# Block 0's weighted sums over channels: from VectorE to TensorE, with diagonal matrices from ScalarE

## The chip, the cores and the metric

The kernel runs on one core of one Trainium2 chip. The metric is the time of one execution on the device, in microseconds (us). The engines are called by their names: TensorE (PE in the rows; PEld is its weight load), VectorE (DVE), ScalarE (ACT), GpSimd (POOL) and SyncE (SP). Each runs its own list of instructions in order, and they wait for each other at semaphores.

## What is computed

A transformer layer with a residual of four channels: attention, then an MLP, then a layer with a matrix of signs. What matters here is the MLP's read. Ahead of it the residual is updated channel by channel with the attention's output (`rat_write`), and the read makes two outputs, each a weighted sum over the four channels with its own weight for each feature, normalized over the features:

```python
def rat_read(res, W, gamma, beta, num_outputs):
    b, l, _ = res.shape
    x = res.reshape(b, l, H, C)                # H = 512 features, C = 4 channels
    y = jnp.einsum('blhc,hoc->bloh', x, W)     # num_outputs = 2 in the MLP
    mu = y.mean(-1, keepdims=True)
    var = y.var(-1, keepdims=True)
    yn = (y - mu) * jax.lax.rsqrt(var + EPS)
    yn = yn * gamma.reshape(num_outputs, H) + beta.reshape(num_outputs, H)
    return yn.reshape(b, l, num_outputs * H)
```

There are 2 x 1024 tokens. Everything is f32; the large products are made from a high and a low part in a rounded f32 format.

## The kernel before

Features lie on the 128 partitions, tokens along the free axis. The tokens are worked in `NB` = 4 blocks of `T` = 512. The program has four phases: setup, read, attention, and `block_phase`, to which the change belongs. In `block_phase` each block `v` has a **first write** (update of the residual with the attention's output, then the read), an **inner product** (`inner`: gate and up projections, product, down projection, 16 steps), a **second write** (update with the MLP's output) and the product with the signs (`signs`). For blocks 1 to 3 the first write is laid between the steps of another block's products by the class `Between`. For block 0 there is no other work: its first write stands alone, after the attention and ahead of `inner(0)`.

The order in each engine is the order in which the Python generators issue. Block 0's first write goes like this:

- TensorE: `expansions` (factors for the update, banks `X0` and `X1`), then `walls(1)` (60 matmuls that belong to block 1 and fill banks 0 to 4 of the eight PSUM banks), then `read(0)`: for each of the two outputs `o` the mean over features (matmuls of `ones_h` with `Y`, line 1657), then the same with the squares for the variance (line 1666).
- VectorE: `factors`, then for each channel `c` the update in `channel` (lines 2052 to 2060, for the last channel 2067 to 2072) on a piece `hidden` of 128 x 2048, and behind it the sums: eight instructions of 128 x 512, one for each of two outputs and four groups `hc` of 128 features, which multiply the piece by the weight `RW[:, hc, o, c]` and add it to `Y` (lines 2109 and 2111). Behind channel 2 stands `small_lows` (line 2080), which frees the bank `SMALL` (4). At the end `Y - mean` (2122), times the reciprocal deviation (2127), gamma and beta (2130), and the low part `ZL` (2136).
- ScalarE: the exponentials of the update (1870), `take_walls(1)`, which copies banks 0 to 3 to `out_1` (1890), four weight DMAs for `inner(0)` (1903 to 1908), of which the first waits for the last update (`wr` 4), and the third for the store of channel 2's piece and the sums of channel 2 (`y` 3); then squares (1911), reciprocal deviation (1918, 1920), the high part `ZH` (1926).
- GpSimd: loads and stores of the pieces. Block 0 has three buffers for four channels, so channel 3's load (line 1430) waits for the store of channel 0's piece and for channel 0's sums (`y` 1). The stores of channels 1 to 3 (line 1436) stand behind it in the queue.

Semaphores: `wr` counts updated pieces, `y` the sums (channels 0 to 2, then output 0 and output 1 of the last), `ym` means, `yc` subtractions, `sq` squares, `yv` variances, `rs` reciprocal deviations.

## Time and profile before

| | us |
|---|---|
| median of 3 runs | 2212.17 |
| lowest and highest of them | 2210.51, 2214.36 |
| the profiled execution's own time | 2214.25 |
| its span (first to last instruction) | 2212.4 |
| mean granted TensorE clock | 0.959 of full speed |

The profile is of one execution. All starts and durations are read from it, in us from the start of its span. What lies around the span (2214.25 against 2212.4) is not seen in it. The chain of waits is the path that ended last, followed back from the last instruction; a wait that is not on it costs nothing. The granted clock is TensorE's: 1.00 is 2.4 GHz, 0.50 is 1.2 GHz, and a value between them is a slice in which it changed.

### The profile page before, as it was taken

The page shows a single profiled execution, that of the slowest core. Times are in us where ns is not written, and L with a number is a line of the kernel's source. Part 1 is how long each engine was busy: PE and PEld are TensorE (multiplying, and loading weights), DVE is VectorE, ACT ScalarE, POOL GpSimd, SP SyncE. Part 2 cuts the span into 40 slices and gives each one's busy share as a digit, 9 for nine tenths or more (in the row PEclk, how much of TensorE's full clock was granted, in tenths as well). Part 3 has the DMA queues.
Part 4 walks back from the last instruction along what each step waited for, and adds up shares of the span by engine and source line. Part 5 has one row for each costly group of instructions (what it writes and reads, how often), then busy time and mean ns, then how long its engine had stood idle before and what let it go on. Part 6 is the DMA issues. An engine that isn't in the chain of part 4 may idle for free.

```text
span 2212.4 us, 25095 instructions
## 1 busy us (share of the span) xinstructions
PE 1981.1 (90%) x9562; PEld 1378.9 (62%) x9562; DVE 1415.1 (64%) x1563; ACT 978.9 (44%) x1376; POOL 423.3 (19%) x325
## 2 busy tenths in 40 slices
PE   2789897999999996289989999999999999989997
PEld 0344456666566553157767777777777677766786
DVE  3677767677777755958657638758639658468100
ACT  3656652787788875044145233143341162431100
POOL 1000004676555550000000001110001000011111
PEclk9899997999999997699999999999999999999999
DMA  8848346686666743246666657777658677559675
GB/s 198 186 110 187 91 102 207 238 289 235 239 239 223 265 171 128 100 165 235 230 238 225 248 186 218 233 243 261 227 191 234 207 263 277 224 162 258 156 183 136
DMA packets 180924, 453.87 MB, mean 205 GB/s; under 512 B 64320, under 2 KB 64576, under 8 KB 165440
## 3 DMA queue, kind: packets, MB, share of 16 engines
q1 hardware_dynamic: 146160, 313.31, 42.3%
q0 software_dynamic: 32480, 128.46, 20.9%
q10 hardware_dynamic: 2160, 10.43, 1.3%
q8 instruction: 79, 1.29, 0.2%
q14 instruction: 45, 0.37, 0.1%
HBM read 304.80 MB, written 147.32 MB: 204 GB/s over the span
## 4 chain that ended last, share of the span: by engine, by line
PE 44%; DVE 7%; DMA 5%; ACT 4%; issue 2%; SPq 0%; POOL 0%; DVEq 0%; POOLq 0%; ACTq 0%
PE ps L1788 16%; PE ps L1598 8%; PE ps L1600 7%; PE ps L1599 7%; DMA sign_h<-sign_h_scratch 2%; DMA up<-up_s_scratch 2%; PE ps L1657 1%; PE ps L1666 1%; PE ps L1695 1%; ACT L1817 1%; PE ps L1618 1%; DVE Y L2111 1%; PE ps L1707 1%; DVE DL_attn L2018 0%; DVE E_attn L2023 0%
## 5 line engine op out<-in xcount | busy, mean ns | idle before, releaser
L1788 PE MATMUL ps<-XH,sign_h 128*128 128x512 f32 x768 | 308.9, 402 | 13.5 <-DMA sign_h<-sign_h_scratch 8.7
L1788 PE MATMUL ps<-XL,sign_h 128*128 128x512 f32 x768 | 302.9, 394 | 0.0
L1159 DVE TENSOR_REDUCE maxes<-ps 128x1 f32<-128x512 f32 (+3 forms) x384 | 207.8, 554 | 97.4 <-PE ps L972 75.0
L1598 PE MATMUL ps<-ZH,up 128*128 128x512 f32 x512 | 205.3, 401 | 15.5 <-DVE ZL L2136 8.9
L1599 PE MATMUL ps<-ZL,up 128*128 128x512 f32 x512 | 201.0, 392 | 0.0
L1600 PE MATMUL ps<-ZH,up 128*128 128x512 f32 x512 | 200.9, 392 | 0.0
L1086 ACT ACTIVATE probs<-ps 128x512 f32<-128x512 f32 (+3 forms) x384 | 167.5, 485 | 50.6 <-PE ps L999 29.9
L1788 PEld LDWEIGHTS ps<-XH,sign_h 128*128 128x128 f32 x768 | 146.0, 190 | 60.9 <-issue 13.0
L969 PE MATMUL ps<-turned_k,turned_q 96*128 96x512 f32 (+3 forms) x384 | 157.6, 424 | 12.0 <-DVE maxes L1159 10.0
L1015 PE MATMUL ps<-probs,v_ones 128*64 128x512 f32 (+3 forms) x768 | 167.3, 514 | 0.3 <-ACT probs L1086 0.3
L1788 PEld LDWEIGHTS ps<-XL,sign_h 128*128 128x128 f32 x768 | 146.3, 191 | 31.6 <-issue 1.9
L969 PEld LDWEIGHTS ps<-turned_k,turned_q 96*128 96x128 f32 x384 | 75.2, 196 | 121.2 <-DVE maxes L1159 73.5
L1509 POOL DMA_DIRECT2D out<-product_scaled x64 | 55.8, 872 | 440.2 <-DVE product_scaled L2205 439.9
L1598 PE MATMUL ps<-inner_h,proj 128*128 128x512 f32 x320 | 129.3, 404 | 3.5 <-DVE inner_l L2186 3.5
L999 PE MATMUL ps<-turned_q,turned_k 97*128 97x512 f32 (+3 forms) x384 | 126.7, 386 | 0.1
L1598 PEld LDWEIGHTS ps<-ZH,up 128*128 128x128 f32 x512 | 97.1, 190 | 47.1 <-issue 18.4
L1599 PE MATMUL ps<-inner_l,proj 128*128 128x512 f32 x320 | 125.5, 392 | 0.0
L1600 PE MATMUL ps<-inner_h,proj 128*128 128x512 f32 x320 | 125.3, 392 | 0.0
L1974 ACT ACTIVATE silu<-ps 128x512 f32<-128x512 f32 x64 | 38.3, 599 | 181.7 <-PE ps L1600 181.5
L2183 DVE TENSOR_TENSOR product<-ps,silu 128x512 f32<-128x512 f32 x64 | 44.2, 690 | 107.6 <-PE ps L1600 102.3
L1599 PEld LDWEIGHTS ps<-ZL,up 128*128 128x128 f32 x512 | 97.2, 190 | 20.8 <-issue 1.2
L1600 PEld LDWEIGHTS ps<-ZH,up 128*128 128x128 f32 x512 | 97.0, 189 | 20.8
(334 smaller groups left out, 4169.4 us busy)
## 6 DMA issues: line engine op xcount, KB each, us to landing
sign_h<-sign_h_scratch SPq DMA_DIRECT2D x256, 256.0 KB, 3.8
up<-up_s_scratch SPq DMA_DIRECT2D x58, 1024.0 KB, 6.4
proj<-proj_s_scratch SPq DMA_DIRECT2D x58, 640.0 KB, 4.1
X<-in_x POOLq DMA_DIRECT2D x16, 1024.0 KB, 15.4
xn_scratch<-X SPq DMA_DIRECT2D x16, 1024.0 KB, 14.2
sign_raw<-in_sign SPq DMA_DIRECT2D x32, 512.0 KB, 7.9
sign_h_scratch<-sign_high SPq DMA_DIRECT2D x32, 512.0 KB, 4.0
sign_l_scratch<-sign_low SPq DMA_DIRECT2D x32, 512.0 KB, 5.3
```

The lines of the kernel that those rows point to most:

```text
L969: mm = eng.matmul(ps[:, bank, 0:w], ST[0][n % 3][e][0:STACK, q * P:(q + 1) * P], ST[1][n % 3][e][0:STACK, k0:k0 + w], start=True, stop=not ...
L999: mm = eng.matmul(ps[:, SC + e, 0:w], ST[1][v % 3][e][:, k * P:(k + 1) * P], ST[0][v % 3][e][:, q0:q0 + w], start=True, stop=not diag, ski ...
L1015: mm = eng.matmul(ps[64 * e:64 * e + 2 * HD, O[h], c:c + w], VO[v % 2][:, k, e], PT[p % NPT][:, e, 0:w], start=k == 0, stop=p + 1 == last_ ...
L1086: eng.activation(PT[p % NPT][:, e, 0:w], ps[:, SC + e, 0:w], ACT.Exp, scale=HD ** -0.5).then_inc(ex.sem, ex.unit)
L1159: eng.tensor_reduce(MAXES[:, e, q, k0 // T:k0 // T + 1], ps[:, MX[m % 2], 0:w], AX.X, ALU.max).then_inc(mx_read.sem, mx_read.unit)
L1509: eng.dma_start(io["out"][:, m, tokens(u)], RES[a][:], accum_op=ALU.add).then_inc(out[a].sem, out[a].unit)
L1598: eng.matmul(out_ap, lh, rh, start=start, stop=False, skip_group_check=True)
L1599: eng.matmul(out_ap, lh, rl, start=False, stop=False, skip_group_check=True)
L1600: return eng.matmul(out_ap, ll, rh, start=False, stop=stop, skip_group_check=True)
L1788: mm = eng.matmul(ps[:, sign_bank(m)], s[q][:, f], x[:, n], start=n + w == 0, stop=n == NF - 1 and w == len(operands) - 1, skip_group_chec ...
L1974: eng.activation(SG[:], ps[:, X0], ACT.Silu).then_inc(silu.sem, silu.unit)
L2183: TTo(PR[:], ps[:, X1], SG[:], ALU.mult).then_inc(prod.sem, prod.unit)
```

## The change

Block 0's read gets its sums from TensorE. The weight of a feature is the same for all tokens, so a multiplication of 128 features by their weights is a matmul with a diagonal matrix. ScalarE makes the 32 diagonals (four channels, two outputs, four groups) from the identity, each with one ACTIVATE of 128 x 128 and `RW` as its scale, ahead of its third exponential; they lie in 16 KB of the arena `b` (`DIAG`). TensorE multiplies each updated piece with eight of them and adds up over the channels in all eight PSUM banks (`read_sums`, between `walls(1)` and `read(0)`); it waits for `out_1` (banks 0 to 3 copied), and ahead of channel 0's second output for `small_0` (bank 4 read). ScalarE copies the sums to `Y`, four banks at a time, behind its four weight DMAs. VectorE's sums in block 0 go; its `small_lows` moves into channel 1, behind the second of its four steps. The means go to banks 0 and 1. The semaphores `sq` and `rs` become one, `sq_rs`, and `y` is now counted by TensorE (channels 0 to 2) and ScalarE (the two copies). The other blocks are as before.

```diff
--- before.py
+++ after.py
@@ -1312,6 +1312,7 @@
         first = [attn, mlp[0], attn, attn]
         ps = ctx.enter_context(nc.psum_tensor("ps3", [P, 8, 512], F32))
         SMALL, X0, X1, F0 = 4, 5, 6, 7
+        DIAG = in_b("read_diagonals", 0, [P, C, 2, HC, P])
...
-        y, ym, yc, sq, yv, rs, z, zh, zl = (ev("r_" + n, per=k) for n, k in
-            (("y", 5), ("ym", 2), ("yc", 2), ("sq", 2), ("yv", 2), ("rs", 2), ("z", 2), ("zh", 2), ("zl", 2)))
+        y, ym, yc, sq_rs, yv, z, zh, zl = (ev("r_" + n, per=k) for n, k in
+            (("y", 5), ("ym", 2), ("yc", 2), ("sq_rs", 4), ("yv", 2), ("z", 2), ("zh", 2), ("zl", 2)))
+        diagonals_sums = ev("diagonals_sums", per=C + 2)
...
+                def read_sums():
+
+                    s = turn(0, 0)
+                    eng.wait_ge(xr.sem, xr.at(s, 10))
+                    eng.wait_ge(o_0.sem, o_0.at(1))
+                    for c in range(C):
+                        h = pieces(0)[c % len(pieces(0))]
+                        eng.wait_ge(wr.sem, wr.at(s, c + 1))
+                        eng.wait_ge(diagonals_sums.sem, diagonals_sums.at(0, c + 1))
+                        for o in range(2):
+                            if c == 0 and o == 1:
+                                eng.wait_ge(small_0.sem, small_0.at(1))
+                            for hc in range(HC):
+                                mm = eng.matmul(ps[:, o * HC + hc], DIAG[:, c, o, hc], h[:, hc], start=c == 0, stop=c == C - 1)
+                            if c == C - 1:
+                                mm.then_inc(diagonals_sums.sem, diagonals_sums.unit)
+                        if c < C - 1:
+                            mm.then_inc(y.sem, y.unit)
+                        yield
+
                 def read(v):
 
                     eng.wait_ge(xr.sem, xr.at(turn(v, 0), 10))
                     banks = (F0, F0) if v == 1 else (X0, X1)
+                    means = (0, 1) if v == 0 else banks
                     for o in range(2):
                         eng.wait_ge(y.sem, y.at(v, C + o))
                         if v == 1 and o:
                             eng.wait_ge(yc.sem, yc.at(v, 1))
                         for hc in range(HC):
-                            mm = eng.matmul(ps[:, banks[o]], t["ones_h"][:], Y[v][:, o, hc], start=hc == 0, stop=hc == HC - 1)
+                            mm = eng.matmul(ps[:, means[o]], t["ones_h"][:], Y[v][:, o, hc], start=hc == 0, stop=hc == HC - 1)
                         mm.then_inc(ym.sem, ym.unit)
...
                     yield from first_factors(v)
                     if v == 0:
                         yield from walls(1)
+                        yield from read_sums()
                     yield from read(v)
...
                     for c in range(3):
+                        if s == 0 and c == 2:
+                            diagonals()
                         eng.wait_ge(e_in.sem, e_in.at(s, c + 1))
                         table(LOG_EXP)
                         e = (E0, E1)[c % 2]
...
+
+                def diagonals():
+
+                    for c in range(C):
+                        for o in range(2):
+                            for hc in range(HC):
+                                ins = eng.activation(DIAG[:, c, o, hc], t["ident_r"][:].bitcast(F32), ACT.Identity, scale=RW[:, hc, o, c:c + 1])
+                        ins.then_inc(diagonals_sums.sem, diagonals_sums.unit)
...
                         eng.wait_ge(y.sem, y.at(v, 3))
                         eng.dma_start(U[1][:].bitcast(F32), io["up_s"][1]).then_inc(up_in[1].sem, up_in[1].unit)
                         eng.dma_start(W[1][:].bitcast(F32), io["proj_s"][1]).then_inc(proj_in[1].sem, proj_in[1].unit)
+                    for o in range(2 if v == 0 else 0):
+                        eng.wait_ge(diagonals_sums.sem, diagonals_sums.at(0, C + o + 1))
+                        eng.activation(Y[0][:, o], ps[:, o * HC:(o + 1) * HC], ACT.Copy).then_inc(y.sem, y.unit)
                     for o in range(2):
                         eng.wait_ge(yc.sem, yc.at(v, o + 1))
-                        eng.activation(first[v][f"E{o}"][:], Y[v][:, o], ACT.Square).then_inc(sq.sem, sq.unit)
+                        eng.activation(first[v][f"E{o}"][:], Y[v][:, o], ACT.Square).then_inc(sq_rs.sem, sq_rs.unit)
...
                         b = c % len(pieces(v))
                         h = pieces(v)[b]
                         eng.wait_ge(h_in[b].sem, h_in[b].at(0, H_COUNT[v, c]))
+                        if v == 0:
+                            for step, _ in enumerate(channel(s, c, h[:], o_sum, first[v])):
+                                if c == 1 and step == 1:
+                                    small_lows(SM0[1], 1, 0, small_0)
+                                yield
+                            continue
                         yield from channel(s, c, h[:], o_sum, first[v])
                         for o in range(2):
                             for hc in range(HC):
@@ -2114,15 +2157,13 @@
                             if o == 1 and c < C - 1:
                                 eng.wait_ge(y.sem, y.at(v, c + 1))
                             yield
-                        if v == 0 and c == 2:
-                            small_lows(SM0[1], 1, 0, small_0)
...
-                        TTo(y2[:, o], y2[:, o], bc(ps[:, F0 if v == 1 else X0 + o], HC), ALU.subtract).then_inc(yc.sem, yc.unit)
+                        TTo(y2[:, o], y2[:, o], bc(ps[:, (o, F0, X0 + o)[min(v, 2)]], HC), ALU.subtract).then_inc(yc.sem, yc.unit)
```

How the lists of instructions change, with the semaphores that each row waits for. TensorE, from the end of `walls(1)` to the variance; before:

```order
L1599 MATMUL ps<-y_low_10666,wall_a 128x512
L1600 MATMUL ps<-y_high_10667,wall_a 128x512
L1657 MATMUL ps<-Y_10668,ones_h 128x512 [waits s3_r_y,s3_xr]
L1657 MATMUL ps<-Y_10668,ones_h 128x512 x3
L1657 MATMUL ps<-Y_10668,ones_h 128x512 [waits s3_r_y]
L1657 MATMUL ps<-Y_10668,ones_h 128x512 x3
L1666 MATMUL ps<-E_attn,ones_h 128x512 [waits s3_r_sq,s3_r_yc]
L1666 MATMUL ps<-E_attn,ones_h 128x512 x3
L1666 MATMUL ps<-E_attn,ones_h 128x512 [waits s3_r_sq,s3_r_yc]
L1666 MATMUL ps<-E_attn,ones_h 128x512 x3
```

and now:

```order
L1601 MATMUL ps<-y_low_10666,wall_a 128x512
L1602 MATMUL ps<-y_high_10667,wall_a 128x512
L1663 MATMUL ps<-hidden_0_10659,read_diagonals 128x512 [waits s3_wr,s3_diagonals_sums,s3_o_0,s3_xr]
L1663 MATMUL ps<-hidden_0_10659,read_diagonals 128x512 x3
L1663 MATMUL ps<-hidden_0_10659,read_diagonals 128x512 [waits s3_small_0]
L1663 MATMUL ps<-hidden_0_10659,read_diagonals 128x512 x3
L1663 MATMUL ps<-hidden_0_10660,read_diagonals 128x512 [waits s3_diagonals_sums,s3_wr]
L1663 MATMUL ps<-hidden_0_10660,read_diagonals 128x512 x7
L1663 MATMUL ps<-hidden_10658,read_diagonals 128x512 [waits s3_diagonals_sums,s3_wr]
L1663 MATMUL ps<-hidden_10658,read_diagonals 128x512 x7
L1663 MATMUL ps<-hidden_0_10659,read_diagonals 128x512 [waits s3_diagonals_sums,s3_wr]
L1663 MATMUL ps<-hidden_0_10659,read_diagonals 128x512 x7
```

Behind the walls stand 32 matmuls with diagonals, and the mean (with its two rows for each output, now at line 1680) behind these. ScalarE, from the exponentials of block 0's update to the squares; before:

```order
L1870 ACTIVATE E_attn<-E_attn 128x2048 [waits s3_e_in] x3
L1876 ACTIVATE small_1a<-ps,bias_sb 64x512 [waits s3_proj]
L1876 ACTIVATE small_1b<-ps,bias_sb 64x512
L1890 ACTIVATE out_1_10674<-ps 128x2048
L1903 DMA up_10645<-up_s_scratch 128x2048 [waits s3_wr]
L1904 DMA proj_10647<-proj_s_scratch 128x1280
L1907 DMA up_10646<-up_s_scratch 128x2048 [waits s3_r_y,s3_h_out2]
L1908 DMA proj_10648<-proj_s_scratch 128x1280
L1911 ACTIVATE E_attn<-Y_10668 128x2048 [waits s3_r_yc] x2
```

and now:

```order
L1896 ACTIVATE E_attn<-E_attn 128x2048 [waits s3_e_in] x2
L1904 ACTIVATE read_diagonals<-ident_r,read_sb 128x128 x32
L1896 ACTIVATE E_attn<-E_attn 128x2048 [waits s3_e_in]
L1910 ACTIVATE small_1a<-ps,bias_sb 64x512 [waits s3_proj]
L1910 ACTIVATE small_1b<-ps,bias_sb 64x512
L1924 ACTIVATE out_1_10674<-ps 128x2048
L1937 DMA up_10645<-up_s_scratch 128x2048 [waits s3_wr]
L1938 DMA proj_10647<-proj_s_scratch 128x1280
L1941 DMA up_10646<-up_s_scratch 128x2048 [waits s3_r_y,s3_h_out2]
L1942 DMA proj_10648<-proj_s_scratch 128x1280
L1945 ACTIVATE Y_10668<-ps 128x2048 [waits s3_diagonals_sums] x2
L1948 ACTIVATE E_attn<-Y_10668 128x2048 [waits s3_r_yc] x2
```

The diagonals come ahead of the third exponential, the two copies behind the weight DMAs and ahead of the squares. VectorE, from channel 1's update to channel 2's; before:

```order
L2109 TENSOR_SCALAR Y_10668<-hidden_0_10659,read_sb 128x512 x8
L2052 TENSOR_TENSOR OG_attn<-out_sb,RG_attn 128x2048 [waits s3_h_in1,s3_r_y]
L2054 TENSOR_TENSOR hidden_0_10660<-hidden_0_10660,OG_attn 128x2048 [waits s3_dve]
L2057 TENSOR_TENSOR hidden_0_10660<-hidden_0_10660,E_attn 128x2048 [waits s3_rg_e_out,s3_dve]
L2060 TENSOR_TENSOR hidden_0_10660<-hidden_0_10660,OG_attn 128x2048 [waits s3_e_read]
L2111 SCALAR_TENSOR_TENSOR Y_10668<-hidden_0_10660,read_sb,Y_10668 128x512 [waits s3_wr]
L2111 SCALAR_TENSOR_TENSOR Y_10668<-hidden_0_10660,read_sb,Y_10668 128x512 x7
L2052 TENSOR_TENSOR OG_attn<-out_sb,RG_attn 128x2048 [waits s3_h_in2,s3_r_y]
```

and now:

```order
L2089 TENSOR_TENSOR OG_attn<-out_sb,RG_attn 128x2048 [waits s3_h_in1]
L2091 TENSOR_TENSOR hidden_0_10660<-hidden_0_10660,OG_attn 128x2048 [waits s3_dve]
L2117 SCALAR_TENSOR_TENSOR small_1a<-ps,bias_sb,small_1a 64x512 [waits s3_small_high,s3_dve]
L2117 SCALAR_TENSOR_TENSOR small_1b<-ps,bias_sb,small_1b 64x512
L2094 TENSOR_TENSOR hidden_0_10660<-hidden_0_10660,E_attn 128x2048 [waits s3_rg_e_out]
L2097 TENSOR_TENSOR hidden_0_10660<-hidden_0_10660,OG_attn 128x2048 [waits s3_e_read]
L2089 TENSOR_TENSOR OG_attn<-out_sb,RG_attn 128x2048 [waits s3_h_in2,s3_wr]
```

The sums are gone, and the two `small` rows stand between the second and the third step of channel 1.

## Rows read from the trace of the kernel before

**Rows 1.** The page: each engine's busy time, its share of the span, and instructions
```profile
PE 1981.1 (90%) x9562; PEld 1378.9 (62%) x9562; DVE 1415.1 (64%) x1563; ACT 978.9 (44%) x1376; POOL 423.3 (19%) x325
```

**Rows 2.** The chain in order of time, 888 to 945: start us, us, what
```profile
893.14 3.26 DVE Y L2109 x8
...
896.42 2.30 DVE OG_attn L2052
...
905.73 0.05 DVE Y L2111
...
911.15 2.30 DVE OG_attn L2052
...
925.88 0.04 DVE small_1a L2080
...
927.43 2.30 DVE OG_attn L2067
...
934.40 2.75 DVE Y L2111 x4
...
937.29 5.12 PE ps L1657 x8
...
942.43 2.30 DVE Y L2122
```

**Rows 3.** By windows: length, busy (instructions) of each engine, granted clock, DMA share, GB/s
```profile
894.00:899.00 5.00, 0.18 (x1) 0.00 (x0) 4.93 (x9) 4.30 (x4) 0.75 (x1) 1.00 0.37 93
899.00:900.00 1.00, 0.00 (x0) 0.00 (x0) 1.00 (x1) 0.00 (x0) 0.00 (x0) 0.61 0.70 287
...
940.00:941.00 1.00, 1.00 (x4) 0.52 (x3) 0.00 (x0) 0.00 (x0) 0.00 (x0) 0.91 1.00 418
941.00:957.00 16.00, 11.93 (x28) 4.73 (x26) 9.57 (x8) 7.21 (x7) 1.53 (x2) 1.00 0.78 309
957.00:958.00 1.00, 0.00 (x0) 0.00 (x0) 1.00 (x1) 1.00 (x1) 0.00 (x0) 0.63 0.00 0
...
967.00:968.00 1.00, 1.00 (x4) 0.82 (x4) 0.00 (x0) 0.00 (x0) 0.00 (x0) 0.75 0.00 0
```

**Rows 4.** Timeline of TensorE (893.80 to 962.81); chain, second block (1079.37, 1089.19)
```profile
893.80 0.39 PE L1600 MATMUL ps<-y_high,wall_a 128*128 128x512 f32 x1
937.29 8.54 PE L1657 MATMUL ps<-Y,ones_h 128*128 128x512 f32 x16 [43.10 <-DVE Y L2111]
946.81 7.10 PE L1666 MATMUL ps<-E_attn,ones_h 128*128 128x512 f32 x16 [0.98 <-ACT E_attn L1911]
962.81 0.77 PE L1598 MATMUL ps<-ZH,up 128*128 128x512 f32 x1 [8.90 <-DVE ZL L2136]
...
1079.37 3.67 PE ps L1657 x8
...
1089.19 3.43 PE ps L1657 x8
```

**Rows 5.** Timeline of ScalarE around the first write's exponentials; L1086's forms by shape
```profile
863.06 2.56 ACT L1841 ACTIVATE E_attn<-E_attn,du_b_sb 128x512 f32<-128x512 f32 x4
...
880.42 1.91 ACT L1870 ACTIVATE E_attn<-E_attn 128x2048 f32<-128x2048 f32 x1 [0.89 <-DVE E_attn L2038]
893.26 1.92 ACT L1870 ACTIVATE E_attn<-E_attn 128x2048 f32<-128x2048 f32 x1 [10.92 <-DVE E_attn L2064]
...
896.46 1.88 ACT L1890 ACTIVATE out<-ps 128x2048 f32<-128x2048 f32 x1
...
L1086 ACT ACTIVATE probs<-ps 128x128 f32<-128x128 f32 x64 | 15.1, 276 | 5.8 <-PE ps L1002 5.3
```

**Rows 6.** Timeline of GpSimd; times to landing of the loads (L1430) and stores (L1436)
```profile
896.96 0.75 POOL L1430 DMA_DIRECT2D hidden<-xn_scratch  x1 [4.91 <-DVE Y L2109]
...
DMA to landing us min/median/max: 5.4/5.9/7.8
...
DMA to landing us min/median/max: 4.1/4.2/9.8
```

More of the change, by code:

```diff
@@ L1661, in read @@
                         eng.wait_ge(yc.sem, yc.at(v, 2 if v == 1 else o + 1))
-                        eng.wait_ge(sq.sem, sq.at(v, o + 1))
+                        eng.wait_ge(sq_rs.sem, sq_rs.at(v, o + 1))
                         if v == 1 and o:
-                            eng.wait_ge(rs.sem, rs.at(v, 1))
+                            eng.wait_ge(sq_rs.sem, sq_rs.at(v, 3))
                         for hc in range(HC):
@@ L1687, in second_write @@
                     else:
-                        eng.wait_ge(rs.sem, rs.at(1, 2))
+                        eng.wait_ge(sq_rs.sem, sq_rs.at(1, 4))
                     eng.wait_ge(small_1.sem, small_1.at(u))
@@ L1723, in inner @@
                                 eng.wait_ge(zl.sem, zl.at(v, o + 1))
-                                eng.wait_ge(rs.sem, rs.at(v, o + 1))
+                                eng.wait_ge(sq_rs.sem, sq_rs.at(v, o + 3))
                             else:
@@ L1919, in first_write @@
                         eng.wait_ge(chain.sem, chain.next())
-                        eng.activation(R[v][:, o], R[v][:, o], ACT.Exp, scale=-0.5).then_inc(rs.sem, rs.unit)
+                        eng.activation(R[v][:, o], R[v][:, o], ACT.Exp, scale=-0.5).then_inc(sq_rs.sem, sq_rs.unit)
                         yield
@@ L2121, in first_write @@
                         eng.wait_ge(y.sem, y.at(v, C + o))
-                        TTo(y2[:, o], y2[:, o], bc(ps[:, F0 if v == 1 else X0 + o], HC), ALU.subtract).then_inc(yc.sem, yc.unit)
+                        TTo(y2[:, o], y2[:, o], bc(ps[:, (o, F0, X0 + o)[min(v, 2)]], HC), ALU.subtract).then_inc(yc.sem, yc.unit)
                         yield
                     for o in range(2):
-                        eng.wait_ge(rs.sem, rs.at(v, o + 1))
+                        eng.wait_ge(sq_rs.sem, sq_rs.at(v, o + 3))
                         eng.wait_ge(yc.sem, yc.at(v, o + 1))
```

## The prediction

> **What bounds the kernel now.** I read the page first: TensorE is busy for 90% of the span, VectorE for 64%, ScalarE for 44% [rows 1]. So the end is set by TensorE nearly everywhere, and a change that gives TensorE more to do can only pay where TensorE stands idle. I therefore went to the chain of waits and looked for the stretch in which TensorE is not on it. That is block 0's first write. From 893.14 to 937.29 the chain is VectorE alone, one instruction behind the other [rows 2], and the clock table shows TensorE without any work from 894 on [rows 3]; its last wall matmul starts at 893.80 [rows 4]. In that chain each of the four channels has its elementwise update and behind it the weighted sums `Y`, which only VectorE does. After the last sums the chain goes to TensorE for the mean (937.29, 5.12 us) and back to VectorE at 942.43 for the subtraction [rows 2]. From there to the start of the inner product at 962.81 [rows 4] the change touches nothing on the path. So the question is by how much the subtraction at 942.43 starts earlier.
>
> **What leaves VectorE.** Channel 0's sums hold it from 893.14 to 896.42, 3.28 us. Channel 1's from 905.73 to 911.15, 5.42 us, and channel 2's take the same pattern [rows 2]. Together 3.28 + 2 x 5.42 = 14.12 us come out ahead of the last channel's update. The `small_lows` pair (925.88 to 927.43, 1.55 us) is moved from behind channel 2 into channel 1 and stays in the sum. So the updates end at: channel 1, 905.73 - 3.28 + 1.55 = 904.0; channel 2, 913.3; channel 3, 934.40 - 14.12 = 920.3. The fourth sums (934.40 to the mean's start at 937.29, 2.89 us for half of them) leave too.
>
> **What TensorE gets.** 32 f32 matmuls with 512 columns, 8 for each channel. No row shows one with a diagonal, but `ones_h` times `Y` has the same shapes and types, and there a matmul is two records: 8 records (4 matmuls) take 3.43 us at full clock between others, 3.67 us where somebody waits for the end [rows 4]. So a channel costs 2 x 3.43 = 6.86 us at 2.4 GHz. The updates come 9.3 us apart (904.0, 913.3), the last one 7.0 us later, so at full clock TensorE keeps up. Channel 0's sums wait for the copy `out_1`, which ends at 896.46 + 1.88 = 898.34 [rows 5]; they run from 898.4 to 905.5. Channel 1's then run to 912.3, channel 2's from 913.3 to 920.2, channel 3's from 920.3. Behind channel 3's 6.86 us stands the mean of output 0 with 3.67 us: 920.3 + 6.86 + 3.67 = 930.8. The subtraction moves from 942.43 to 930.8, which is **11.6 us**.
>
> **ScalarE's copies.** Each half of the sums is copied from PSUM, priced by `out_1`'s same form at 1.88 us [rows 5]. Output 0's sums end at about 924.0 and its copy at 925.9, before TensorE is through with output 1's at 927.2: the copy is hidden, with 1.3 us to spare. Output 1's copy ends at 929.3, before its mean can start at 930.6. Ahead of the copies ScalarE has to issue four weight DMAs, the first when the last update is done (934.40 before [rows 2], 920.3 now) and two of them once channel 2's piece is stored and its sums are read. The store goes out about 0.6 us behind 913.3 and lands 4.1 to 4.2 us later [rows 6], the sums end at 920.2; so the queue is free about 2 us after 920.3, ahead of 924.0. Cost: nothing, and up to 1 us if these waits end late.
>
> **The diagonals.** ScalarE makes 32 tiles of 128x128 between the exponential that ends at 880.42 + 1.91 = 882.33 and the next one, at 893.26, ahead of which it sat idle for 10.92 us [rows 5]. No row shows this form. The nearest below is the 128x128 exponential from PSUM with 0.276 us: 8.8 us in all, hidden. Above it is the 128x512 exponential with a bias from a tile, four in 2.56 us, 0.64 us each: 20.5 us, which would push everything behind it on ScalarE by 9.6 us. I take 0.30 us, near the lower row, since the tile has a quarter of the upper one's columns (0.30 x 32 = 9.6 us, so 1.3 us of the idle time is left). The Trainium skill (ScalarE: Activation LUTs, What ACT_TABLE_LOAD costs) gives an ACTIVATE 186 ns and 0.833 ns for each column, 93 ns for an operand that is a pointer, and 93 ns of overlap; by that a diagonal is estimated at 0.29 us and the gain stays whole, where by the upper row only about 3 us of it would be left. The rows bear out that price at 512 columns (0.64 us for each of four).
>
> **A transfer that now waits for TensorE.** Channel 3's piece goes into channel 0's buffer, and its load waits for channel 0's sums. Before, these were done at 896.40 and the load was issued at 896.96; it landed 5.4 us later, others took up to 7.8 us [rows 6]. Now the sums end at 905.5, the load goes out at 906.1 and lands between 911.5 and 913.9. VectorE wants the piece at 913.3. Behind it on GpSimd's queue stands the store of channel 1's piece (ready at 904.0), which will share the engines with it. So the stall is 0 to 0.6 us; the cover of 12 us that this load had has shrunk to about 1 us. I take nothing for it in the sum.
>
> **The clock.** TensorE's last work before the sums starts at 893.80. The granted clock stays at 1.00 until 899 and falls in the slice after it; in another place TensorE was idle from 953.9 and the clock fell between 957 and 958 [rows 3, 4]. The sums begin at 898.4, after 4.2 us of idle, so they may begin at either level. Both times that TensorE came back cold in this stretch the full clock was there 2.9 us (937.29, up in the slice from 940) and 4.7 us (962.81, up in the slice from 967) later [rows 3, 4]. A cold start costs half of that, 1.5 to 2.3 us, on channel 0 alone; TensorE has nothing to catch up by channel 3 (1.7 us more: 907.2, 914.1, 920.9, against 920.3), but the load above then lands at 913.2 to 915.6 and stalls VectorE by 0 to 2.3 us. In return the mean now comes on a warm TensorE: its 5.12 us become 3.67, which is in the sum already. The later cold start before 962.81 stays; it may end sooner or later by up to 0.9 us.
>
> **Rivals.** (a) *The load is late.* TensorE starts channel 0 cold, the load lands by up to 2.3 us after VectorE wants it, and the gain is 9 to 11 us: 2201 to 2203 us. For it speaks that the clock fell after an idle time shorter than 4.2 us once; against it that it held for more than 4.2 us the other time.
> (b) *TensorE stays at half clock, and the kernel gets slower.* The work now comes in bursts with a wait ahead of each. At 1.2 GHz a channel is 13.7 us, four in a row from 898.4 end at 953.3, and with a cold mean (6.9 us) the subtraction starts at 960.1: 17.7 us later, 2230 us. It decides from the point where the four channels together take over 40.6 us, which is some 26 us at the low level. Against it: the gaps are 0.9 us and nothing, the granted clock did not move over the 0.98 us of idle that lie between the mean's and the variance's matmuls in the window from 941 to 957 [rows 3], and it rose in under 5 us both times. [...]
> (c) *The diagonals are dear.* At over 0.34 us each they push the copy `out_1`, the `small` halves and so channel 0's sums; at 0.64 us the gain is 3 us, 2209 us; over 0.73 us it is gone.
> (d) *The gain is taken back downstream.* The inner product that starts at 962.81 is bound by TensorE, with everything around it released by TensorE or by this same stretch, so I see nothing at a fixed time. If there is something, the result is near 2212 us.
>
> **How the numbers follow.** Differences under 0.2% (4.4 us) can't be told from no change. The profiled execution has a span of 2212.4 us and took 2214.25 us, 1.85 us around it. 2214.25 - 11.6 = 2202.65 for an execution like it; it lay 2.1 us over the median of the runs, 2212.17, so against the median the forecast is 2212.17 - 11.6 = **2200.6 us**. Chances: 0.60 for the forecast (a gain of 10.8 to 12.6 us with the clock's 0.9 us), 0.23 for (a), 0.06 for (c), most of which is still faster, 0.06 for (d), 0.05 for (b) and other losses. The range reaches below by the 0.9 us of the clock and the 2 us by which the runs differ, and above over (a) with the same scatter and into (c): 2197 to 2206. Faster 0.89, same 0.07, slower 0.04.
>
> **What would show it.** In the profile after: VectorE's updates of channels 1 to 3 end at about 904, 913 and 920, with no idle time ahead of channel 3's first product (if there is, released by a DMA, (a) holds); 16 records for each channel on TensorE in 6.9 us, channel 0's from 898.4; the diagonals done before 893; the subtraction at 930.8 and the inner product at 951.2; the span 2200.8. The forecast is wrong if TensorE's records in this stretch lie 0.85 us apart beyond channel 0, if ScalarE's exponential moves away from 893.3, or if the stretch ends at 951 and the span is not shorter by the same amount.

## The result and the profile after

The changed kernel is faster by about ten microseconds, a gain of about the size forecast, but the predicted time and its range lay too low.

| | median us | runs | ratio to the kernel before, 95% interval |
|---|---|---|---|
| kernel before, beside the changed one | 2216.11 | 8 | |
| changed kernel | 2206.01 | 8 | 0.996 [0.9943, 0.9978] |
| changed kernel, repeated (label `again`) | 2205.99 | 7 | 0.9945 [0.9925, 0.9966] |
| changed kernel, repeated (label `again2`) | 2202.95 | 6 | 0.9934 [0.9912, 0.9956] |

All three intervals lie below 1. The differences of the medians are 10.1, 10.3 and 13.2 us; the forecast was 11.6 us. The three runs of before on which the prediction leaned had a median of 2212.17 us; with more runs it is 2216.1 us (8, these three among them), 2216.3 (24), 2215.6 (17) and 2216.1 (17).

The profiled execution of the changed kernel is a long one: it took 2217.9 us, where six of the other seven took 2204.6 to 2207.2. Its first 960 us serve for the stretch in question; for the rest other traces were taken. The page of the changed kernel (engines: busy us, share, instructions), which answers [rows 1]:

```profile
span 2216.1 us, 25229 instructions
...
PE 2014.5 (91%) x9626; PEld 1393.5 (63%) x9626; DVE 1397.5 (63%) x1531; ACT 991.6 (45%) x1410; POOL 423.2 (19%) x325
```

TensorE has 64 records more (32 f32 matmuls of two records), VectorE 32 instructions less, ScalarE 34 more. The chain in order of time in the stretch, which answers [rows 2] (start us, us, what):

```profile
899.59 8.77 PE ps L1663 x16
908.39 0.52 issue
908.92 7.27 DMA hidden<-xn_scratch
916.28 2.30 DVE OG_attn L2104
918.61 2.30 DVE OG_attn L2107
920.93 2.30 DVE hidden L2109
923.28 7.13 PE ps L1663 x16
930.42 3.45 PE ps L1680 x8
933.94 2.30 DVE Y L2163
```

This is another chain than the one forecast. It does not come along VectorE from channel to channel. It comes from TensorE's sums of channel 0, through GpSimd's queue and the load of channel 3's piece, and only then to VectorE. Behind the last update the order is as forecast: sums of channel 3, mean, subtraction.

The whole stretch lies later in this trace by 1.17 us for a reason ahead of it: channel 0's first product starts at 882.79, before at 881.62. Counted from that product, the subtraction moved from 60.8 us (942.43 - 881.62) to 51.2 us (933.94 - 882.79), which is 9.7 us, and the start of the inner product from 81.2 to 71.5 us, again 9.7 us. A second trace of the kernel before (label `before_again`) has 61.9 and 82.3 us; against it both gains are 10.8 us.

GpSimd's timeline (answers [rows 6]: the load L1432 behind the sums, the stores L1438) and VectorE's wait for it:

```profile
908.92 0.75 POOL L1432 DMA_DIRECT2D hidden<-xn_scratch  x1 [15.71 <-PE ps L1663]
909.67 0.56 POOL L1438 DMA_DIRECT2D h_scratch<-hidden  x1
```

```profile
916.28 2.29 DVE L2104 TENSOR_TENSOR OG_attn<-out_sb,DL_attn 128x2048 f32<-128x2048 f32 x1 [1.87 <-DMA hidden<-xn_scratch]
```

The load went out 12 us later than before (896.96 in [rows 6]) and took 7.3 us, with the store of channel 1's piece right behind it. VectorE waited 1.87 us.

ScalarE's timeline, which answers [rows 5]:

```profile
883.41 9.48 ACT L1904 ACTIVATE read_diagonals<-ident_r,read_sb 128x128 f32<-128x128 f32 x32
894.41 1.91 ACT L1896 ACTIVATE E_attn<-E_attn 128x2048 f32<-128x2048 f32 x1 [1.53 <-DVE E_attn L2101]
...
927.02 1.88 ACT L1945 ACTIVATE Y<-ps 128x2048 f32<-128x2048 f32 x1 [27.53 <-PE ps L1663]
930.45 1.88 ACT L1945 ACTIVATE Y<-ps 128x2048 f32<-128x2048 f32 x1 [1.56 <-PE ps L1663]
```

The 32 diagonals took 9.48 us, 0.30 us each, and 1.53 us of idle time were left ahead of the exponential. Output 0's copy (927.02 to 928.90) ended 1.5 us before TensorE was through with output 1's sums (930.42). The granted clock by windows, which answers [rows 3] (length, busy PE, PEld, DVE, ACT, POOL, clock, DMA share, GB/s):

```profile
895.00:899.00 4.00, 0.00 (x0) 0.00 (x0) 3.93 (x3) 3.96 (x4) 0.00 (x0) 1.00 0.33 131
899.00:902.00 3.00, 2.41 (x3) 1.18 (x4) 2.96 (x3) 0.49 (x1) 0.00 (x0) 0.58 0.03 5
902.00:903.00 1.00, 1.00 (x2) 0.34 (x1) 0.97 (x2) 0.00 (x0) 0.00 (x0) 0.54 0.00 0
903.00:908.00 5.00, 5.00 (x13) 2.28 (x12) 4.93 (x3) 0.00 (x0) 0.00 (x0) 1.00 0.01 2
```

TensorE had been idle since the end of the walls (4.66 us of "issue" ahead of 899.59). In this trace the clock fell to 1.2 GHz as the sums began and was back at 2.4 GHz at about 903. So channel 0's 16 records took 8.77 us, where channel 3's took 7.13 us with the latency at the end. What this document calls the cold start is this stretch at 1.2 GHz near the start of a burst.

### The profile page after: what moved, and what is told of

Its sections match the earlier page's. It is cut to its first block, busy times and chain, and to the rows that moved or that the text cites. A ratio compares the mean times of both kernels' runs of the same rounds, so it can differ in the third digit from the quotient of the medians.

```text
span 2216.1 us, 25229 instructions
## 1 busy us (share of the span) xinstructions
PE 2014.5 (91%) x9626; PEld 1393.5 (63%) x9626; DVE 1397.5 (63%) x1531; ACT 991.6 (45%) x1410; POOL 423.2 (19%) x325
## 4 chain that ended last, share of the span: by engine, by line
PE 44%; DMA 7%; DVE 5%; ACT 4%; issue 2%; SPq 0%; POOL 0%; DVEq 0%; POOLq 0%; ACTq 0%
PE ps L1812 15%; PE ps L1600 8%; PE ps L1601 8%; PE ps L1602 8%; DMA sign_h<-sign_h_scratch 4%; DMA up<-up_s_scratch 2%; PE ps L1680 1%; PE ps L1689 1%; PE ps L1620 1%; ACT L1841 1%; PE ps L1731 1%; PE ps L1663 1%; PE ps L1719 1%; ACT E_attn L1865 0%; DVE E_attn L2060 0%
## 5 line engine op out<-in xcount | busy, mean ns | idle before, releaser
L1600 PE MATMUL ps<-ZH,up 128*128 128x512 f32 x512 | 206.3, 403 | 19.1 <-DMA up<-up_s_scratch 10.1
L1086 ACT ACTIVATE probs<-ps 128x512 f32<-128x512 f32 (+3 forms) x384 | 167.4, 486 | 50.9 <-PE ps L999 29.8
```

Source lines behind the costliest of these rows:

```text
L1086: eng.activation(PT[p % NPT][:, e, 0:w], ps[:, SC + e, 0:w], ACT.Exp, scale=HD ** -0.5).then_inc(ex.sem, ex.unit)
L1600: eng.matmul(out_ap, lh, rh, start=start, stop=False, skip_group_check=True)
```

## The experiments

Three things were open: whether the load, TensorE's cold start or both cost the 1.9 us on the path; whether the stretch passes its gain on to the end one to one; and whether the long execution shows a cost of the change in later stages. Each trace gave two numbers that do not depend on where in the span the stretch lies: the time from channel 0's first product of VectorE to the subtraction, and to the first matmul of the inner product.

| label | to the subtraction | to the inner product | wait for the load | median us (runs) | ratio [95%] |
|---|---|---|---|---|---|
| before | 60.8 | 81.2 | none | 2216.11 (8) | |
| before_again | 61.9 | 82.3 | none | 2214.17 (10) | 0.999 [0.9979, 1.0001] |
| changed kernel | 51.2 | 71.5 | 1.87 | 2206.01 (8) | 0.996 [0.9943, 0.9978] |
| again | 51.2 | 71.6 | 1.92 | 2205.99 (7) | 0.9945 [0.9925, 0.9966] |
| again2 | 50.9 | 71.3 | 1.65 | 2202.95 (6) | 0.9934 [0.9912, 0.9956] |
| fourth | 49.7 | 70.1 | none | 2203.87 (6) | 0.9933 [0.9911, 0.9956] |
| warm | 49.3 | 69.7 | none | 2205.7 (12) | 0.9959 [0.9942, 0.9976] |
| delay | 61.4 | 84.1 | 2.84 | 2219.32 (12) | 1.0005 [0.9989, 1.0021] |
| split | 47.4 | 67.8 | 1.58 | 2203.03 (7) | 0.9941 [0.9919, 0.9962] |
| split_fourth | 46.2 | 66.6 | none | 2205.62 (5) | 0.9945 [0.9924, 0.9965] |
| best | 45.8 | 66.2 | none | 2198.54 (4) | 0.9908 [0.9891, 0.9926] |
| best2 | 45.8 | 66.2 | none | 2202.19 (6) | 0.9921 [0.9895, 0.9947] |
| twice | 58.7 | 79.1 | 2.95 | 2215.2 (10) | 0.9992 [0.9973, 1.0011] |

In `delay` the first subtraction starts after the extra work.

### again: the changed kernel, repeated

No edit.

> The changed kernel as it is, timed again beside the kernel before, with a new trace. Theory (the gain is what block 0's first write gives, 9.7 us to the start of the inner product in the trace after, and what the trace lost behind it was that one execution): the median lies 9 to 11 us under that of before, and the trace ends near 2204 us with the later stages as long as before. Rival (the change costs something later, 1 to 6 us in the inner products of blocks 1 to 3): the trace again shows these stages longer than before, and the gain is 4 to 7 us.

The median lies 10.3 us under that of before. The stretch repeats to 0.1 us. From the first `silu` to the last product of the signs it took 1234.1 us (before: 1232.4), so the 1245.1 us of the first trace are not the change's. In that long execution the fourth block's inner product took 151.1 us from its first `silu` to its last, here 144.9. The windows over that stage, first of the long execution, then of this one:

```profile
1770.00:1925.00 155.00, 149.77 (x660) 113.97 (x658) 100.99 (x77) 65.54 (x68) 7.05 (x10) 0.98 0.66 244
```

```profile
1767.00:1915.00 148.00, 145.91 (x656) 111.12 (x655) 100.51 (x76) 65.72 (x68) 7.13 (x11) 1.00 0.69 255
```

The clock was not at its high level throughout, and TensorE waited longer for the weights: in these groups of TensorE's by line (busy, mean ns, idle before and its releaser) 4.7 us against 1.5 us. This stage accounts for 6.2 of the 11.0 us by which the long execution's part behind the first `silu` is longer; the rest is not broken down.

```profile
L1600 PE MATMUL ps<-ZH,up 128*128 128x512 f32 x128 | 52.3, 408 | 4.7 <-DMA up<-up_s_scratch 4.7
```

```profile
L1600 PE MATMUL ps<-ZH,up 128*128 128x512 f32 x128 | 50.8, 397 | 1.5 <-DMA up<-up_s_scratch 1.5
```

The theory holds for the median. It missed in the trace's end (2206.3 against 2204), which lies within what these stages scatter.

The clock did not fall at the same point as in the first trace. Here the sums began at 900.21 at full clock, and it fell some 1.2 us into them (in the windows the granted clock is the third figure from the end):

```profile
900.00:901.00 1.00, 0.79 (x2) 0.49 (x3) 0.98 (x2) 0.11 (x1) 0.00 (x0) 1.00 0.00 0
901.00:902.00 1.00, 1.00 (x3) 0.49 (x2) 0.97 (x2) 0.00 (x0) 0.00 (x0) 0.72 0.00 0
902.00:904.00 2.00, 2.00 (x3) 0.71 (x3) 1.97 (x2) 0.00 (x0) 0.00 (x0) 0.50 0.03 8
904.00:905.00 1.00, 1.00 (x3) 0.35 (x2) 1.00 (x1) 0.00 (x0) 0.00 (x0) 0.57 0.02 8
905.00:906.00 1.00, 1.00 (x4) 0.52 (x3) 0.97 (x2) 0.00 (x0) 0.00 (x0) 1.00 0.00 0
```

The cost was the same: the load went out 9.38 us after the sums' start, in the first trace 9.33 us.

### fourth: a buffer of its own for channel 3's piece

```diff
-        HID_0 = [in_s("hidden0_0", 0, ...), in_x("hidden1_0", 24, ...), HID[2]]
+        HID_0 = [in_s("hidden0_0", 0, ...), in_x("hidden1_0", 24, ...), HID[2], in_s("hidden3_0", 8, [P, HC, T])]
...
+                        elif v == 0 and c == 3:
+                            eng.wait_ge(yl.sem, yl.at(1))
...
-                    for c in (1, 2):
+                    for c in (1, 2, 3):
                         load_h(0, c)
                     store_h(0, 0)
-                    load_h(0, 3)
```

The rest of the edit counts the fourth buffer's transfers and lets block 1's loads wait for its store.

> Channel 3's piece gets a buffer of its own (the place of y_raw, free by then), so its load no longer waits for channel 0's sums. Theory (the wait for the load cost 1.9 us on VectorE's path): no idle time ahead of channel 3's first product, and because TensorE then has a backlog of 0.7 us by channel 3, the subtraction comes 1.2 to 1.9 us earlier than in the changed kernel, as does the end. Rival (TensorE's cold start is what costs, the load only hides it): under 0.5 us.

VectorE had no idle time ahead of channel 3. The subtraction came 1.5 us earlier, as the theory had it with TensorE's backlog: its 64 records ran without a gap from 900.44, in 29.4 us, past the end of VectorE's last update.

```profile
900.44 29.40 PE L1665 MATMUL ps<-hidden,read_diagonals 128*128 128x512 f32 x64 [4.39 <-issue]
```

The median was 2.1 us lower than that of `again` on the same chip, but the intervals of the two overlap.

### warm: TensorE kept busy up to the sums

```diff
                         yield from walls(1)
+                        for _ in range(20):
+                            eng.matmul(ps[:, F0], WA[:, 0, 0, rows(0)], YH[1][:, 0], start=True, stop=True)
                         yield from read_sums()
```

> 20 more matmuls of 128x512, whose results nobody reads, fill TensorE's idle time between block 1's walls and the diagonal sums. Theory (channel 0's sums took 8.8 us instead of 6.9 because TensorE started them at half clock, and that made the load late): channel 0's sums take 6.9 us, the load goes out 1.8 us earlier, the wait for it on VectorE falls from 1.9 us to under 0.5 us, and the end comes 1.4 to 1.9 us earlier. Rival (the load is late because it shares the engines with the store): the wait stays over 1 us.

TensorE's timeline:

```profile
891.96 4.70 PE L1700 MATMUL ps<-y_high,wall_a 128*128 128x512 f32 x20
896.59 13.97 PE L1663 MATMUL ps<-hidden,read_diagonals 128*128 128x512 f32 x32
```

Two channels' sums took 13.97 us, 7.0 us each, and the granted clock was 1.00 in the whole window from 890 to 908. The load went out 7.7 us after the sums' start instead of 9.3 us, and landed after 6.8 us instead of 7.3 us; VectorE did not wait at all. So the cold start made the load late: with the same buffer, the same wait and the same store behind it, 1.65 us less on TensorE, and the faster landing, took away all 1.9 us. The rival, by which the wait would stay over 1 us, falls as the whole explanation. It does not fall as a part of it: with the 5.4 us that the load took in the kernel before, it would have landed at 914.3 in the first trace (908.92 + 5.4), just before VectorE was free at 914.41, even after the cold start. So the wait needed both, the cold start and the longer landing. How much of that is due to the store behind the load no run shows. The subtraction came 1.85 us earlier. The median of twelve runs is only 0.3 us below `again`'s; a difference of this size these medians don't resolve.

### delay: 9.3 us put back

```diff
+                    for _ in range(4 if v == 0 else 0):
+                        eng.wait_ge(ym.sem, ym.at(0, 1))
+                        og = attn["OG"]
+                        in_turn(TTo(og[:], og[:], og[:], ALU.add))
                     for o in range(2):
                         eng.wait_ge(ym.sem, ym.at(v, o + 1))
```

> The changed kernel with four additions of 128x2048 on VectorE, whose results nobody reads, between the first mean and the first subtraction: 9.3 us put back on the path at the end of the stretch. Theory (what the stretch gains or loses reaches the end one to one): 9 to 9.5 us slower than the changed kernel, so within 1.5 us of the kernel before. Rival (later stages take back a part of any gain): less than 7 us slower.

It was 13.3 us slower than `again`, more than theory and rival said. The trace shows why: the inner product started 12.5 us later, not 9.3.

```profile
950.29 9.35 PE L1689 MATMUL ps<-E_attn,ones_h 128*128 128x512 f32 x16 [10.35 <-ACT E_attn L1948]
```

The extra work gave TensorE 10.35 us of idle time ahead of the variance, so these 16 records took 9.35 us on a cold engine, where they take 7.1 us ([rows 4]), which is 2.2 us more. The rest, 0.9 us, does not come from the additions: it is a longer wait for the load, ahead of them. In this trace TensorE was idle for only 3.51 us ahead of the sums, but the clock fell about 1 us before they began and was back only at about 907.0, 5.8 us into them.

```profile
900.00:901.00 1.00, 0.00 (x0) 0.00 (x0) 0.96 (x2) 1.00 (x1) 0.00 (x0) 0.61 0.00 0
901.00:906.00 5.00, 4.71 (x6) 2.16 (x7) 4.92 (x4) 0.19 (x1) 0.00 (x0) 0.50 0.02 5
906.00:907.00 1.00, 1.00 (x2) 0.36 (x2) 0.97 (x2) 0.00 (x0) 0.00 (x0) 0.50 0.00 0
907.00:908.00 1.00, 1.00 (x3) 0.38 (x2) 1.00 (x1) 0.00 (x0) 0.00 (x0) 0.98 0.00 0
```

The expectation's 9.3 us was wrong because it left out the clock. As far as one trace and these medians tell, nothing is taken back later.

### before_again: the kernel before, traced again

No edit.

> The kernel before, with a new trace. Theory (the stages behind the stretch take the same time in both kernels, and the trace after was one long execution): from the first silu to the last product of the signs it takes 1232 to 1235 us again, as in the repeat of the changed kernel (1234.1 us), and the time is 2214 to 2219 us. Rival (the changed kernel pays 1 us or more there): under 1232 us.

From the first `silu` to the last product 1232.8 us. Two traces of before (1232.4, 1232.8) stand against `again` (1234.1) and `again2` (1229.8), and the other kernels but the long execution lie between 1229.3 and 1235.4 us. Both expectations of the theory were met. No cost of the change in later stages is to be seen, and one under some 3 us could not be. The mean came on a colder TensorE than in the first trace: the 16 records of the means took 9.63 us, before 8.54 us ([rows 4]).

```profile
937.79 9.63 PE L1657 MATMUL ps<-Y,ones_h 128*128 128x512 f32 x16 [42.06 <-DVE Y L2111]
```

### split: output 0's last sums stay on VectorE

```diff
-                        for o in range(2):
+                        for o in range(c == C - 1, 2):
...
+                            if c == C - 1:
+                                eng.wait_ge(y.sem, y.at(0, C - 1))
+                                for hc in range(HC):
+                                    ins = STT(y2[:, 0, hc], h[:, hc], RW[:, hc, 0, c:c + 1], ps[:, hc], ALU.mult, ALU.add)
+                                ins.then_inc(y.sem, y.unit)
```

ScalarE then copies output 1 only.

> The changed kernel, but channel 3's sums of output 0 stay on VectorE, which adds them to the PSUM banks' sums of channels 0 to 2 and writes Y; TensorE makes only output 1's. Theory (behind the last update TensorE alone sets the pace, 6.9 us of sums and 3.5 us of mean, while VectorE idles 10.7 us): four instructions, 2.8 us, lie beside TensorE's 3.5 us for output 1, so the subtraction comes 3.3 to 3.5 us earlier than in the changed kernel, and the end too. Rival (the copy or VectorE's PSUM reads take the place): under 2 us.

The subtraction came 3.8 us earlier, of which 0.3 us is the shorter wait for the load. VectorE's four instructions took 2.72 us, beside TensorE's eight records.

```profile
921.21 2.72 DVE L2150 SCALAR_TENSOR_TENSOR Y<-hidden,read_sb,ps 128x512 f32<-128x512 f32 x4
```

```profile
921.23 3.70 PE L1663 MATMUL ps<-hidden,read_diagonals 128*128 128x512 f32 x8 [0.86 <-DVE hidden L2110]
924.77 7.03 PE L1680 MATMUL ps<-Y,ones_h 128*128 128x512 f32 x16
```

The theory holds in the stretch. The median is 3.0 us under that of `again`, but on another chip.

### split_fourth and best: the edits together

`split_fourth` has the edits of `fourth` and `split`, `best` those of `warm` as well.

> Both: channel 3's piece with its own buffer and output 0's last sums on VectorE. If the two gains are independent: 1.5 us (measured for the buffer up to the subtraction) and 3.4 us, 4.9 us earlier than the changed kernel. If TensorE's backlog after its cold start then counts: 3.9 to 4.5 us.

> As the one before with the 20 filling matmuls as well. With a buffer of its own the load is out of the way, so the cold start can cost only by TensorE's backlog at channel 3: theory 0.4 to 0.9 us better than without the filling matmuls, 5.3 us earlier than the changed kernel at the subtraction; the rival (the clock matters only through the load) expects no difference.

`split_fourth` reached the subtraction 4.9 us earlier than the changed kernel (46.2 against 51.2 us, rounded), at the value for independent gains. Ahead of its four sums VectorE waited 0.84 us for TensorE's sums of channel 2, which is the backlog; in `best` that wait was 0.32 us and the subtraction 5.3 us earlier. So the cold start is worth 0.4 us once the load is out of the way, the lower end of the theory's 0.4 to 0.9. The medians do not follow in this order: 2205.62 us from five runs for `split_fourth` and 2198.54 from four for `best`.

### twice: each diagonal made twice

```diff
+                                eng.activation(UNREAD[:, c, o, hc], t["ident_r"][:].bitcast(F32), ACT.Identity, scale=RW[:, hc, o, c:c + 1])
                                 ins = eng.activation(DIAG[:, c, o, hc], ...)
```

> ScalarE makes each diagonal twice, once into a tile that nobody reads: 32 more ACTIVATEs of 128x128, 9.5 us by the trace after, where 1.5 us of idle time were left. Theory (the diagonals are free only as long as they fit ahead of the third exponential): that exponential, the small halves and out_1 move by 8.0 us, VectorE waits 6.8 us ahead of its small pair, channel 0's sums end 8 us later and the load's wait grows by about 1.2 us, so the subtraction comes 7.5 to 8.5 us later than in the changed kernel, and nearly all of the gain is gone (2 us left at the end). Rival (ScalarE's delay is taken up by the slack of the sums): under 5 us.

The chain moved as expected. ScalarE's exponential started 7.7 us later (902.01 in this trace, 894.41 in the changed kernel's, and channel 0's first product at 882.66 and 882.79), with nothing idle ahead of it, and VectorE waited ahead of its small pair and for the load:

```profile
905.29 0.74 DVE L2119 SCALAR_TENSOR_TENSOR small_1a<-ps,bias_sb,small_1a 64x512 fp32r<-64x512 f32 x1 [6.51 <-ACT small_1b L1912]
...
923.71 2.29 DVE L2106 TENSOR_TENSOR OG_attn<-out_sb,DL_attn 128x2048 f32<-128x2048 f32 x1 [2.95 <-DMA hidden<-xn_scratch]
```

6.51 us, and 1.1 us more for the load, are the 7.6 us by which the subtraction came later, and the kernel was not measurably faster than before. (Beside `again2` on the same chip its median is 12.3 us higher, more than the 7.8 us in the stretch; these ten runs scatter over 17 us.) This gives rival (c) its price: the diagonals have 1.5 us of cover, and behind that each microsecond of ScalarE costs about one.

### again2 and best2: side by side

> The changed kernel once more, as the measure for the one that follows: 2204 to 2207 us, 9 to 11 us under the kernel before.

> All three edits once more beside the changed kernel on the same chip. In the traces the subtraction came 5.3 us earlier than in the changed kernel; theory (one to one to the end): 4.5 to 6.5 us under it, 2199 to 2202 us. Rival (the first result of this kernel, 2198.5 us from four runs, was partly chance and the later stages take some back): 2 to 4 us under it.

In the stretch `best2` repeated `best` to 0.1 us and was 5.1 us ahead of `again2`. In the time it was 0.8 us ahead (2202.19 against 2202.95 us, six runs each). Neither expectation of `best2` was met, and `again2` came out lower than forecast. Over both comparisons the kernel with all three edits has ten runs with a median of 2199.8 us, the changed kernel 21 runs with 2205.8 us. That points to a gain, but the two sets are from different chips, and the one direct comparison does not show it. Both are clearly faster than the kernel before. Whether the three edits are worth their 5 us at the end stays open.

## Why the prediction was right or wrong

**What bounds the kernel** was right: VectorE's sums stood alone on the path, and taking them off moved the end. `delay` is the test of the latter.

**What leaves VectorE** was right to 0.1 us. From channel 0's first product the updates were forecast to end at 22.4, 31.7 and 38.7 us for channels 1 to 3 (904.0, 913.3, 920.3 less 881.6). They ended at 22.4, 31.6 and 40.5 us (905.14, 914.4, 923.25 less 882.8). The last of them is late by the 1.87 us of the wait.

**What TensorE gets** was right at the warm level: 7.13 + 3.45 us, 10.6 together, against a forecast 10.5 us. **ScalarE's copies** and **the diagonals** cost nothing, as forecast, with 0.30 us for a diagonal. Here the trace agrees with the price that the Trainium skill gives (ScalarE: Activation LUTs, What ACT_TABLE_LOAD costs), by which it was estimated at 0.29 us.

**Two terms of the sum failed:** the wait for the load, put at nothing, and the reference from which the gain was taken off. The mechanism was right.

**A transfer that now waits for TensorE** is the step that failed in the gain: "I take nothing for it in the sum". It cost 1.87 us, and 1.6 to 2.8 us in the four other traces that are the same up to there (`again`, `again2`, `split`, `delay`). The text had worked out how it would come about, as case (a): a cold start of 1.5 to 2.3 us on channel 0 (measured 1.65 to 1.9: the load's issue behind the sums' start, 9.33 against 7.68 us in `warm`, or 8.77 - 6.86), a landing time of up to 7.8 us (7.3), a wait of 0 to 2.3 us. What was wrong was the weight: 0.60 for "no wait" and 0.23 for (a). The loss was not an accident of one execution: TensorE was idle for 3.5 to 4.7 us ahead of the sums in seven traces (the changed kernel, `again`, `again2`, `fourth`, `split`, `split_fourth`, `delay`), and in each the clock fell to 1.2 GHz. The question whether the sums begin at either level was the wrong one, though: in `again` they began at full clock and lost as much, because the clock fell behind their start. With the measured wait in the sum the forecast gain would have been 9.7 us; the stretch gave 9.7 us against the first trace of before and 10.8 us against the second, whose mean ran longer at half clock. `warm` shows that without the cold start there is no wait, and `fourth` that the load is the way by which it reached the path; the longer landing, 7.3 us instead of 5.4 us, was needed for the wait too. The prediction's reading that this load had a cover of 12 us before is also wrong: it landed at 902.4 (896.96 + 5.4 [rows 6]), and VectorE took up the piece at 927.43 [rows 2], 25 us later.

**The later cold start** was allowed 0.9 us either way and gave back 0.7 us in the first trace: the clock was up 3.3 us after the inner product's first matmul (954.33, then 957.65 in the chain), before 4.7 us.

```profile
957.23 0.43 PE ps L1600
957.65 0.24 PE ps L1601
```

It reads as scatter and not as a gain of the change: the first `silu` came 5.8 us after that matmul in the first trace, but 6.4 us in `again`, and 6.5 and 6.8 us in the two traces of before.

**The predicted time and the range** failed above all by the reference. The gain was taken off 2212.17 us, the median of three runs, while the kernel before takes 2216 us. 3.9 us of the 5.4 us between 2200.6 and 2206.01 come from this. The other 1.5 us are the difference of the gains, 11.6 against 10.1 us; the wait of 1.9 us is of that size, but the medians do not resolve it. The range allowed 2 us for the scatter of the runs, but the three shown were all on the low side of what longer series give (medians 2215.6 to 2216.3 us, single runs 2207 to 2227 us). The range ended at 2206, just below the measured median. With 2216.11 us as the reference the same working gives 2204.5 us and a range to 2210.

**The rivals.** (a) happened, with its gain of 9 to 11 us; its times of 2201 to 2203 us are low by the same reference. (b), a slower kernel through a clock that stays low, did not: beyond channel 0 the clock was up, and channel 3's sums ran at full speed behind 1.20 us of idle time. The Trainium skill (TensorE: Matmul & The Clock Gate, Loop structure matters more than you think) shows a long wait for a DMA ahead of every matmul as what leaves TensorE cold. The traces agree where the idle time was long, 4.66 us ahead of the first sums and 10.35 us ahead of the variance in `delay`; the short gaps between the channels are not such waits. (c) did not happen, and `twice` showed its price; the 0.73 us for a diagonal from which the gain was to be gone is somewhat too high, as at twice 0.30 us only 2.1 us of it were left in the stretch (60.8 against 58.7): the sum had started from 11.6 us, and the wait for the load grows too. (d) is not seen: from `best` to `delay` the start of the inner product moves by 17.9 us (66.2 to 84.1), the medians by 17 to 21 us. For steps of 5 us and less the medians do not show whether they pass on one to one.

## What to carry to other kernels

Work that was moved to an idle TensorE ran into its low clock here, 1.7 us in channel 0's sums, and what it released was late by that. So look at everything that waited for the old engine's result, the reload of a buffer above all, and not only at the next step of the computation. A buffer whose load had landed 25 us ahead of its use became critical when the reader of its old contents changed. And take a forecast off a reference that is as well known as the gain you want to see: three runs that agreed within 4 us had a median 4 us off that of longer series.

## What the runs showed of the hardware that was not expected

Executions of one kernel on one core scatter by 6 to 17 us here (2207 to 2223 us in 24 runs of before). In the traces the part behind the first `silu` took 1229 to 1235 us, once 1245 us; in the stage compared above the long one had longer waits for weights and a granted clock of 0.98 instead of 1.00.

The clock fell at very different distances behind the same last matmul of the walls: in `delay` 2.4 us behind its end, in the changed kernel's first trace 4.6 us, in `again` and in the trace of before ([rows 3, 4]) some 5 us. So it can fall while the next burst is already running: in `again` 1.2 us into it, in `again2` and `split_fourth` about 1 us into it. It was back 3.3 to 5.8 us after the start of the sums in the seven traces. So a full clock at the first matmul of a burst does not mean that the burst was free of the loss.

And work put on VectorE's path cost more than its own time: 9.3 us of additions made the stretch 11.6 us longer, 2.2 us of it through TensorE's clock.
